# Two attentions, a projection and a mixture of experts on one core: first operands loaded a stage earlier, statistics per block, the last softmax sums on TensorE

## The reference

```python
# layer 0, mixer: linear attention over rotated q, k; kept for later as `mix`
lin = (elu(rope(q) * s) + 1) @ kv / denom @ W_out
# layer 0, branch: layernorm, causal softmax attention with 16-wide heads, Wproj,
# then top-2 of 8 experts with a capacity, gelu, scatter back
# layer 1: layernorm, causal softmax attention with 32-wide heads, Wo,
# times silu(x @ (int4(kernel) + a @ b) + bias), plus x
scores = einsum('bqhd,bkhd->bhqk', q, k) / sqrt(hd)
scores = where(causal, scores, -1e9)
out = einsum('bhqk,bkhd->bqhd', softmax(scores), v)
```

## Time and profile before

| | |
|---|---|
| median of 3 runs | 3089.22 us (3086.56 to 3089.31) |
| the profiled execution, its own time | 3095.93 us |
| span of that execution | 3093.9 us |
| mean granted clock of TensorE in it | 0.953 |
| busy in the span | PE 2860.0, DVE 2024.4, ACT 1520.0, POOL 931.0 us |

### The profile page before, as it was taken

The page is one execution under the profiler, slowest core; times in us unless marked ns, Lnnn a source line. Parts: engine busy times, 40 slices in busy tenths (PEclk is TensorE's granted clock), DMA queues, the critical chain, the costliest instruction groups (busy, mean ns, idle before and its releaser), DMA issues. The chain is left out here.

```text
span 3093.9 us, 46487 instructions
## 1 busy us (share of the span) xinstructions
PE 2860.0 (92%) x18025; PEld 1327.8 (43%) x18025; DVE 2024.4 (65%) x4462; ACT 1520.0 (49%) x2473; POOL 931.0 (30%) x420
## 2 busy tenths in 40 slices
PE   7998999999999982999999999799999999999987
PEld 4664333333333341666666745323333333333326
DVE  6886889989999636000001665588887877878723
ACT  3432467767777741222221444245556565565560
POOL 0001000000000021201000430166777777777780
PEclk9997799999999985999999999799999999999998
DMA  3223221122101033322211354422020220211005
GB/s 123 79 61 90 46 39 29 33 46 49 42 21 41 12 94 116 83 61 92 65 48 50 123 180 140 111 51 48 23 62 12 66 62 8 66 35 39 8 11 173
DMA packets 143626, 196.08 MB, mean 63 GB/s; under 512 B 14000, under 2 KB 109056, under 8 KB 141472
## 3 DMA queue, kind: packets, MB, share of 16 engines
q1 hardware_dynamic: 130304, 170.77, 20.0%
q0 software_dynamic: 6144, 16.79, 2.3%
q10 hardware_dynamic: 6960, 5.58, 0.6%
HBM read 116.81 MB, written 75.76 MB: 62 GB/s over the span
## 5 line engine op out<-in xcount | busy, mean ns | idle before, releaser
L912 ACT ACTIVATE at_probs<-at_st 128x512 f32<-128x512 f32 (+3 forms) x1280 | 589.0, 542 | 446.5 <-PE at_st L998 284.2
L874 POOL TENSOR_TENSOR at_probs<-at_probs 128x2048 f32<-128x2048 f32 (+3 forms) x208 | 732.9, 3528 | 223.7 <-ACT at_probs L912 137.1
L383 DVE TENSOR_REDUCE at_part<-at_s 128x1 f32<-128x512 f32 (+3 forms) x1280 | 689.3, 602 | 76.7 <-PE at_s L421 35.0
L365 ACT ACTIVATE at_probs<-at_st 128x1024 f32<-128x1024 f32 (+3 forms) x640 | 541.6, 895 | 285.2 <-PE at_st L440 143.8
L938 DVE TENSOR_REDUCE at_part<-at_s 128x1 f32<-128x512 f32 x768 | 498.5, 683 | 69.8 <-PE at_s L990 65.9
L990 PE MATMUL at_s<-at_kT,at_qT 96*128 96x512 f16 (+3 forms) x1280 | 391.3, 361 | 29.7 <-DMA at_kT<-klo 10.5
L998 PE MATMUL at_st<-at_qT,at_kT 98*128 98x512 f16 (+3 forms) x1280 | 380.5, 357 | 15.6 <-ACT at_probs L912 10.5
L421 PE MATMUL at_s<-at_kT,at_qT 48*128 48x512 f16 (+3 forms) x1280 | 363.3, 370 | 24.8 <-DMA at_kT<-klo 10.2
L932 DVE CUSTOM_DVE_ANT_0 at_s<-at_s,at_later 128x384 f32<-128x384 f32 (+3 forms) x512 | 246.8, 498 | 110.8 <-PE at_s L990 110.2
L507 PE MATMUL at_acc<-at_probs,at_v 128*32 128x512 f32 (+3 forms) x2560 | 309.9, 558 | 8.9 <-ACT at_otile L352 8.8
L2319 DVE TENSOR_TENSOR ex_ot<-ex_bank,lin_b 128x512 f32<-128x512 f32 x32 | 22.1, 692 | 438.7 <-PE ex_bank L2349 438.7
(11 more groups left out here) (322 smaller groups left out, 3234.0 us busy)
## 6 DMA issues: line engine op xcount, KB each, us to landing
att<-at_otile SPq DMA_DIRECT2D x64, 256.0 KB, 2.1
lin_w<-in_W SPq DMA_DIRECT2D x16, 1024.0 KB, 7.6
at_v<-v SPq DMA_DIRECT2D x14, 1024.0 KB, 14.6
v<-pr_vt SPq DMA_DIRECT2D x32, 256.0 KB, 3.3
exp_out<-ex_ot SPq DMA_DIRECT2D x32, 256.0 KB, 2.1
v<-p_vt SPq DMA_DIRECT2D x32, 256.0 KB, 3.5
fi_a<-att SPq DMA_DIRECT2D x8, 1024.0 KB, 6.3
at_qT<-qhi SPq DMA_DIRECT2D x14, 512.0 KB, 9.5
```

Of the source, the lines that this page charges most:

```text
L365: act.activation(probs[:, quad % RING, heads_down * p:heads_down * (p + 1), off:QB], st_ps[n % st_slots][:, :, off:QB], ACT.Exp, scale=EXP ...
L383: dve.tensor_reduce(part[:, w % 2, qt * HG + h, j:j + 1], s_ps[n % S_SLOTS][:, 0:width], AX.X, ALU.max).then_inc(item_free, 1)
L874: pool.tensor_tensor(total, total, probs[:, slots.slot[quad], :, off:QB], ALU.add).then_inc(add_done, 1)
L912: act.activation(probs[:, slots.slot[quad], h, off:QB], st_ps[n % ST_SLOTS][:, off:QB], ACT.Exp, scale=EXP_SCALE).then_inc(exp_done, 1)
```

## The change

It has five parts.

- **Statistics per block.** `groups_of` is gone. Block b counts block b + 2 between `feat` and `lo q`, ACT takes its Sqrt at the end of block b, and DVE makes the root at the start of block b + 1, before it normalises. int4 levels and low-rank product move from block 2 to block 6. Some tiles share memory now.
- **Narrow attention.** q and k of group 0 and their shift rows are loaded at the start of block 4 of `project_first`, after all stores of blocks 0 to 3 have landed; the masks are made by POOL in that stage too. Group 1's shift rows are issued at the stage's start; its operands, as before, behind the strip of unit 1. What was issued between the strips of unit 0 and unit 1 (all but the rest of v) is gone.
- **Wide attention.** q, k, v of group 0 are loaded in block 4 of `combine_and_project`, in the same way, into tiles that live on (`Carried`).
- **Last sums.** In the last unit, (7, 0), POOL adds nothing: each of its 4 key steps is a set of its own, and PE sums it. ACT now waits for `pv_done` also before it overwrites the first step of a set.
- **Finish.** Wo and the first four blocks of att are loaded into the memory of group 6's operands once group 6 is done. The loops are unrolled, and multiply, add and store take 2 row tiles at a time (4 stores in flight) where they took 1, 1 and 4.

```diff
@@ project_first @@
-    NPRE, NLORA = 0, 2
-    groups_of = [(0, 1), (1, 2), (2, 4), (4, NB)]
-    counted_in = {1: 2, 2: 3}
+    NPRE, NLORA = 0, 6
...
+                if b == NQB:
+                    sp.wait_ge(v_kept, 64 * NQB)
+                    sp.wait_ge(qk_kept, 64 * NQB)
+                    load_first(sp)
...
             pool.partition_all_reduce(redall[:, :], red[:, :], P, bass.bass_isa.ReduceOp.max).then_inc(all_s, 1)
+            masks.make(pool)
...
                 if b + 1 < NB:
                     h_rows(b + 1)
+                if b + 2 < NB:
+                    deviation(b + 2)
...
             for b in range(NB):
-                if b > 1 and b + 1 < NB:
+                if b and b + 1 < NB:
+                    root(b + 1)
                     normalise(b + 1)
...
-                if b in counted_in:
-                    statistics(counted_in[b])
...
                 step(f"feat {b}", stt(out=feat[:, :, :], in0=feat[:, :, :], scalar=1.0, in1=pos[:, :, :],
                                       op0=ALU.min, op1=ALU.add))
+                if b + 2 < NB:
+                    statistics(b + 2)
                 if b == NLORA:
+                    levels()
@@ narrow_attention, tensor @@
-            pe.wait_ge(wide_ready, 6)
+            pe.wait_ge(masks.ready, 6)
...
+            pe.wait_ge(first_ld, FIRST_LOADS)
@@ wide_schedule and wide_attention @@
-def summed_sets(u):
+def summed_sets(u, last=False):
+    if last:
+        return (1,) * (4 * u + 4)
     return ((4,), (2, 2, 4), (4, 2, 2, 4), (4, 2, 2, 2, 2, 4))[u]
...
+    def load_group(self, eng, C, qk, v):
+        K = 32
+        for dst, src, r in ((self.q, qk[0][0], 0), (self.k, qk[1][0], 0), (self.q, qk[0][1], 1),
+                            (self.k, qk[1][0], 1), (self.q, qk[0][0], 2), (self.k, qk[1][1], 2)):
+            eng.dma_start(dst[r * K:(r + 1) * K, :, :], src[0].rearrange("h d t -> d h t")).then_inc(self.group_ld, 16)
...
+    def load_finish(self, eng, W, att):
+        eng.dma_start(self.w, W["Wo"].rearrange("(g p) n -> p g n", p=P)).then_inc(self.w_ld, 16)
+        for blk in range(NB // B):
+            self.load_value(eng, att, blk)
...
+                    elif g + 2 == GROUPS:
+                        sp.wait_ge(pv_done, quads_done[ev[1]])
+                        for k in range(2):
+                            sp.wait_ge(out_stored[k], issued[k])
+                        carried.load_finish(sp, W, out)
...
             pe.wait_ge(C["const_ready"], C["const_count"])
+            pe.wait_ge(carried.group_ld, Carried.GROUP_LOADS)
...
                     pe.wait_ge(add_done, slots.add_of[slots.last[totals]])
+                    pe.wait_ge(exp_done, HG * (slots.last[totals] + 1))
                     for h in range(HG):
-                        mm = pe.matmul(sum_ps[32 * h:32 * h + 32, :], C["ones32"][:, :],
-                                       probs[:, slots.slot[slots.first[totals]], h, :],
+                        mm = pe.matmul(sum_ps[32 * h:32 * h + 32, off:QB], C["ones32"][:, :],
+                                       probs[:, slots.slot[slots.first[totals]], h, off:QB],
@@ combine_and_project, sync @@
+                if b == NQB:
+                    sp.wait_ge(part_out, 64 * NQB)
+                    sp.wait_ge(v_kept, 64 * NQB)
+                    carried.load_group(sp, C, qk_out, v_out)
@@ finish @@
-            sp.dma_start(a[0][:, :, :], rows[0, :, :, 0:QB]).then_inc(ld[0], 16)
-            sp.dma_start(w[:, :, :], W["Wo"].rearrange("(g p) n -> p g n", p=P)).then_inc(w_ld, 16)
-            for blk in range(1, NB):
...
+            for blk in range(NB // B, NB):
+                pe_s.wait(sp, f"x {2 * (blk - NB // B) + 1}")
+                carried.load_value(sp, att, blk)
```

More of the change, by code:

```diff
@@ L601, in released @@
             n = slots.set_of[old]
-            return sum_end[n] if n < len(sum_end) else None
+            return max(sum_end[n], pv_end[old]) if n < len(sum_end) and old < len(pv_end) else None
         n = slots.add_of[old] - 1
@@ L1469, in deviation @@
             def deviation(n):
-                a, e = groups_of[n]
+                cols = slice(4 * n, 4 * n + 4)
                 dve_s.wait(act, f"moments {n}")
-                step(f"sqrt {n}", act.activation(std[:, :, 4 * a:4 * e], var[:, :, 4 * a:4 * e], ACT.Sqrt))
+                step(f"sqrt {n}", act.activation(std[:, :, cols], var[:, :, cols], ACT.Sqrt))
             def xn_rows(b):
@@ L2798, in _ @@
         @block.scalar
         def _(act):
-            def body(blk, k, i):
-                dve_s.wait(act, "add3", blk)
-                act.dma_start(out.rearrange("b (n p) d -> p (b n) d", p=P)[:, bass.ds(blk * 4, 4), :],
-                              o[k][:, :, :]).then_inc(stored[k], 16)
-            blocks(act, body)
-            for k in range(2):
-                act.wait_ge(stored[k], 1 + 16 * NB // 2)
+            rows = out.rearrange("b (n p) d -> p (b n) d", p=P)
+            for n in range(PAIRS):
+                dve_s.wait(act, f"add {n}")
+                act.dma_start(rows[:, 2 * n:2 * n + 2, :], o[:, n % 4, :, :]).then_inc(stored[n % 4], 16)
@@ L2826, in _ @@
-            blocks(dve, body)
+            for n in range(PAIRS):
+                tile, rows = o[:, n % 4, :, :], slice(2 * n, 2 * n + 2)
+                if n >= 4:
+                    dve.wait_ge(stored[n % 4], 16 * (n // 4))
+                pe_s.wait(dve, f"x {n}")
+                dve_s.step(f"mul {n}", dve.tensor_tensor(tile, banks.tile(f"x {n}")[:, :, :], g_all[:, rows, :], ALU.mult))
+                dve_s.wait(dve, f"mul {n}")
+                dve_s.step(f"add {n}", dve.tensor_tensor(tile, tile, x_all[:, rows, :], ALU.add))
@@ L2828, in _ @@
         @block.tensor
         def _(pe):
-            pe_s.start(pe)
-            pe.wait_ge(w_ld, 16)
-            def body(blk, k, i):
-                pe.wait_ge(ld[k], i * 16 + 16)
-                for t in range(4):
-                    d = banks.take(pe, f"x{t}", blk)
+            pe.wait_ge(carried.w_ld, 16)
+            for n in range(PAIRS):
+                blk = n // 2
+                k = blk % (NB // B)
+                if n % 2 == 0:
+                    pe.wait_ge(carried.a_ld[k], 16 * (blk // (NB // B) + 1))
+                d = banks.take(pe, f"x {n}")
+                for y in range(2):
+                    t = 2 * (n % 2) + y
@@ L2837, in body @@
                     for g in range(4):
-                        mm = pe.matmul(d[:, 0:D], a[k][:, g, t * P:(t + 1) * P], w[:, g, :],
-                                       start=g == 0, stop=g == 3)
-                    pe_s.step(f"x{t}", mm)
-            blocks(pe, body, NB // B)
+                        mm = pe.matmul(d[:, y, :], a[k][:, g, t * P:(t + 1) * P], w[:, g, :], start=g == 0, stop=g == 3)
+                pe_s.step(f"x {n}", mm)
 def build(nc, W, x, out):
```

439 lines of the change are left out of this document (170 added, 269 removed).

## The result

The changed kernel takes 3049.82 us, the kernel before 3089.22 in the same comparison: 39.4 us less, at a ratio of 0.9873, 95% interval 0.9854 to 0.9893. The 3049.82 is the median of four executions, one of which took 4003 us at a mean granted clock of 0.646; the interval leaves that one out, and the median of the three others (3048.66 to 3050.56) is 3049.08, 40.1 us less. The profiled execution of the changed kernel took 3049.08 us (span 3047.3), so it stands at the median of the three, where that of before stood 6.7 us above.

A forecast was written before the change was run, and what follows sets the result against it. PE, busy for 92% of the span, was taken as the bound, with gains only from its standstills or low clock. Terms 12.5 + 5.3 + 6.2 + 5.3 + 7.3 + 0.5 = 37.1 us, from 3089.22 to 3052.1 us; range 3041 to 3068.

The forecast's parts named there:

- In block 0 there was no gap before `lo q`: +1.4: Block 0 of `project_first`: the added statistics find no idle time of DVE before `lo q` and cost 1.4 us.
- Masks: nine short POOL instructions: `project_first`: masks made by POOL after its last duty in the stage cost nothing.
- The low-rank product, "+1.5": `project_first`: the low-rank product with its two transposes is not saved but paid in block 6, +1.5 us.
- The slack of 0.3 to 0.4 us: Blocks 1 to 5 of `project_first`: added DVE work fits with this slack before PE waits; 0 to +1.5 us per block.
- The rival in which DVE becomes the bound: `project_first`: slack missed, PE waits for `fv` or `sum` in blocks 1 to 5; 3059.6 us, at most 3072; chance 0.16.
- The row on the price of a table switch: ACT in `project_first`: Exp starts 1.30 us after a table load, so a switch costs its 1.28 us and no more.
- The starts: Narrow and wide attention start earlier, -5.3 and -6.2 us; rival: starts give nothing, 11.5 lost, 3063.6 us, chance 0.08.
- The early loads: Rival in `combine_and_project`: wide attention's 4 MB delay block 4's stores, 5 us lost once, 3057 us; chance 0.04.
- The prediction's 5.3: Wide attention's end: the last sum ends 5.3 us earlier, including about 1.5 us more PE work for four narrow sums.
- A slice count at 0.7 other than three: Sign of error, whole kernel: the number of profile slices with granted clock 0.7 should stay three.
- the stretch unchanged within 2 us: Sign in each attention: time from first maximum to last product stays the same within 2 us.
- rival of the clock: Attention starts: shorter gaps keep PE's clock up, 17 us less, 3035, chance 0.06; or two slices worse, 3096, chance 0.03.

## Why the prediction was right, point by point

**The sum held.** 37.1 us were forecast, the medians say 39.4, and 44.6 and 39.6 on two other chips. The terms that the change makes by itself, as measured, come to a little less: 11.4 for the statistics and masks, 5.3 for the narrow start, 6.1 for the wide one, 5.2 for the last sums net of their work, 7.2 and 0.4 for `finish` make 35.6. So the mechanisms are right, and that the total came within 2.3 us owes something to luck: the statistics gave less than forecast, and the weight load below gave 2 us that nobody had forecast. What is left between the terms and the medians, 2 us here and 7 on one chip, is not explained. The 46.6 us between the two profiled spans hold more, and most of the more is not the change's: the narrow attention of the profile before happened to run in the slower course of the clock.

**Statistics per block: 12.5 forecast, 11.4 measured.** Blocks 1 and 2 gave 15.4, as forecast. The terms that failed are small ones. "In block 0 there was no gap before `lo q`: +1.4" is about 1.55, of which the wait before `sum` is 1.29: behind its first 16 wide matmuls the block takes 30.19 us in the kernel before, and 31.76 and 31.74 in the two kernels that have the new statistics but not the masks in this stage. With the masks it takes 32.14, and these 0.4 us belong to a step that the prediction put at nothing, "Masks: nine short POOL instructions". While POOL makes them, DVE's normalisation takes 0.3 us longer. The changed kernel, and the one with the narrow start undone:

```profile
37.53 1.68 DVE L1513 TENSOR_SCALAR pr_z<-all_x_all,pr_mean,pr_rstd 128x256 f32<-128x256 f32 x4 [0.15 <-PE pr_bank L1648]
```

```profile
36.94 1.38 DVE L1560 TENSOR_SCALAR pr_z<-all_x_all,pr_mean,pr_rstd 128x256 f32<-128x256 f32 x4 [0.15 <-PE pr_bank L1695]
```

Then `vB` waits 1.35 us instead of 0.95. The normalisation takes 1.67 to 1.69 us in all ten profiles with the masks in this stage and 1.38 in the four without; what the two engines contend for is not shown. The low-rank product, "+1.5", is 2.05 in block 6: PE is busy for 1.65 us more than in block 5 and waits 0.40 for a bank ahead of `fqk`. The rest of the 2.2 us is the first 16 wide matmuls, 8.62 us against 7.62, which take 7.6 to 9.0 us in the fourteen profiles.

**The slack of 0.3 to 0.4 us existed.** It was the boldest number of the prediction, and 0.3 and 0.5 us were measured, by pushing on it at two places, ahead of the root and ahead of `sum`. The rival in which DVE becomes the bound was half a microsecond of DVE per block away. The row on the price of a table switch was right to go by. By the figure of the Trainium skill (ScalarE: Activation LUTs, What ACT_TABLE_LOAD costs), an estimate, the root would have been 1.4 us later and the blocks 1 us longer; they kept their 27.82.

**The starts** gave 5.3 and 6.1 us and nothing was absorbed: from first maximum to last product the wide attention changed by 0.4 us. Undone one at a time they cost 4.7 and 5.4. The early loads held up neither stores (the later blocks of `combine_and_project` keep their pace with and without them) nor, as far as the stretch's length tells, strips.

**Last sums: the mechanism is right.** The last sum's distance to the last product fell by 6.6 us, and about 1.4 us of the three added sums are paid ahead of it. The prediction's 5.3 took the second part off at the right size.

**The clock: a criterion that failed.** "A slice count at 0.7 other than three" would have been wrong by the prediction's own words, and the page shows one; "the stretch unchanged within 2 us" is wrong in the narrow attention, by 7.5. The step at fault is the silent one of taking one profiled execution's clock as the kernel's. The prediction's rival of the clock ties a change to the shorter gaps, and no run bears that out: the stretch differed by 6 us between kernels with the same gap. Fourteen profiles show the narrow attention at 820.0 to 823.5 us ten times and at 827.2 to 827.9 four times. With a late start or a held one it was 827.6, 822.3, 827.2, 823.5 and 822.4; with an early start 827.9 twice and 820.0 to 822.7 seven times. So neither kernel owns a course. Whether the early start makes the better one more frequent is not shown by so few, and stays open.

**Two microseconds that were not forecast.** Behind the narrow attention PE stands for 8.9 to 10.3 us in the four profiles with the old `narrow_attention`, and for 7.1 to 7.7 in the ten with the new one. PE waits there for the weight of the next stage, `ag_w`, in every one of them. The DMA rows of before (count, KB, median us to landing):

```profile
ag_w<-in_Wproj ACTq DMA_DIRECT2D x1, 256.0 KB, 5.4
```

and of after:

```profile
ag_w<-in_Wproj ACTq DMA_DIRECT2D x1, 256.0 KB, 3.4
```

The same 256 KB, first on their queue in both and issued 3.8 us behind the last product, land in 3.4 instead of 5.4 us; in all fourteen it is 5.1 to 6.4 us with the old `narrow_attention` and 3.2 to 3.9 with the new one. In the old kernel ACT's queue had carried the first keys; that this is the cause was not tried, and it stays open. It is a gain of 2 us that the prediction doesn't have, and with it the measured terms come to 37.6.

## What to carry to other kernels

Where an engine's work is late in a few blocks and idle in the others, cut the work to the blocks' size and lay each piece into the engine's idle time between two things that PE waits for; then measure the slack that is left by doubling one piece, since here it is 0.3 to 0.5 us of 27.8. A first operand that a stage loads for itself costs its whole flight, and no part of that is hidden while every engine waits for it: the three moved loads gave 5.3, 6.1 and 7.2 us, each what its row said. Work that is moved to an idle engine is not free: nine short POOL instructions beside DVE cost 0.4 us here. Before a stretch of a trace is explained by the edit, profile the same program again: one stage of 820 us had two lengths here, some 6 us apart, in kernels that differ only in what comes after it.

## What the runs showed of the hardware

The granted clock at the start of the narrow attention follows one of two courses in thirteen of fourteen profiles. It begins at 0.50 to 0.56 over the first 20 us, which is the lower of its two levels (1.2 GHz of 2.4) for nearly all of the time, after PE has stood for 4.8 to 10.6 us. From 100 us on it stands at 0.66, then 1.00, or at 0.59, then 0.93 and 0.91. The fourteenth, with the narrow start undone (823.5 us), lies between them, at 0.62, then 0.91, 1.00 and 0.91. The Trainium skill (TensorE: Matmul & The Clock Gate, What's actually happening) says that the gate's window runs free and does not start anew with the kernel, so that the point of the rise depends on where the first matmul falls in it; two courses for one program agree with that, though no run here could set the phase. The first 16 wide matmuls of the kernel vary too, by 1.3 us.

While POOL ran the nine instructions that make the masks, four operations of DVE on 128x256 took 1.68 us instead of 1.38.

On three chips DVE, ACT and PE stood for some 7 to 12 us each within the first 24 us of `combine_and_project`, in all twelve profiles, on DVE and ACT mostly with "remote" or "issue" as the releaser, and the stage took 276 to 284 us; on the chip of the first comparison it took 262 to 263, without such a stand. All of the difference lies ahead of DVE's first `p_yt`: what follows takes 178.7 to 179.0 us in all profiles, on all four chips. What holds the engines is not shown.
